# Spiking attention: score units of two full PSUM banks instead of two half-filled ones, clips and spikes dealt out anew over the engines

## The reference

```python
def spike(x):                      # THRE = 4
    return jnp.floor(jnp.clip(x, 0.0, THRE) + 0.5)
B, N, C = x.shape                  # 16, 548, 128
H = 8; hd = C // H; scale = hd ** (-0.5)
...                                # spike, Wqkv, batch norm over all tokens
q = spike(qkv[0]); k = spike(qkv[1]); v = spike(qkv[2])
attn = jnp.einsum('bhnd,bhmd->bhnm', q, k)
attn = spike(attn)
out = jnp.einsum('bhnm,bhmd->bhnd', attn, v) * scale
out = spike(out.transpose(0, 2, 1, 3).reshape(B, N, C))
return jnp.einsum('bnc,dc->bnd', out, Wproj) + bproj
```

## Time and profile before

| | before |
|---|---|
| median of three runs | 2126.67 us (2124.03 to 2128.3) |
| profiled execution, its own time | 2130.16 us |
| its span in the trace | 2128.3 us |
| PE, DVE, ACT, POOL busy over the span | 73%, 62%, 35%, 34% |
| `attend`: first instruction of the block to the last of the residual | 1246.6 to 1650.8 us |
| scores: first and last start | 1258.8 and 1646.7 us |

### The profile page before, as it was taken

The page is one execution under the profiler, slowest core; times in us unless marked ns, Lnnn a source line. Parts: engine busy times, 40 slices in busy tenths (PEclk is TensorE's granted clock), DMA queues, the critical chain, the costliest instruction groups (busy, mean ns, idle before and its releaser), DMA issues. The chain is left out here.

```text
span 2128.3 us, 31340 instructions
## 1 busy us (share of the span) xinstructions
PE 1544.4 (73%) x9132; PEld 1081.9 (51%) x9132; DVE 1318.0 (62%) x2105; ACT 744.3 (35%) x1369; POOL 719.1 (34%) x758
## 2 busy tenths in 40 slices
PE   5779999998701004776627558888888658999998
PEld 3457777775301003555514423333333457788787
DVE  3845555555577892111115777777777657989988
ACT  2235555555300001333203346677666321111111
POOL 1345555552000014788753012222231113323332
PEclk8679999999855556989858889999999859999999
DMA  4050000000210002444450000000000000000000
GB/s 137 0 232 1 0 0 0 0 0 0 74 32 0 1 1 52 85 78 81 64 150 28 4 2 2 0 0 0 0 0 0 1 32 8 11 11 15 11 15 14
DMA packets 69696, 60.85 MB, mean 29 GB/s; under 512 B 15789, under 2 KB 63675, under 8 KB 68363
## 3 DMA queue, kind: packets, MB, share of 16 engines
q1 hardware_dynamic: 52174, 47.52, 6.9%
q0 software_dynamic: 15744, 11.85, 4.1%
q10 hardware_dynamic: 1728, 0.85, 0.1%
HBM read 35.06 MB, written 25.18 MB: 28 GB/s over the span
## 5 line engine op out<-in xcount | busy, mean ns | idle before, releaser
L1610 DVE TENSOR_SCALAR at_clip<-at_slot 128x548 bf16<-128x548 f32 (+1 forms) x320 | 226.4, 722 | 79.7 <-PE at_slot L1453 72.8
L1541 ACT ACTIVATE at_clip<-at_slot,at_four 128x548 bf16<-128x548 f32 (+1 forms) x320 | 226.6, 713 | 126.9 <-PE at_slot L1453 125.0
L1453 PE MATMUL at_slot<-at_qm,at_ks 128*128 128x274 bf16 (+1 forms) x1280 | 216.9, 285 | 55.2 <-ACT at_clip L1541 45.7
L1591 POOL TENSOR_SCALAR at_qm<-at_qs,at_headmask 128x548 bf16<-128x548 bf16 x128 | 97.1, 777 | 360.6 <-DVE at_qs L1619 360.6
L1453 PEld LDWEIGHTS at_slot<-at_qm,at_ks 128*128 128x128 bf16 (+1 forms) x1280 | 90.7, 97 | 150.4 <-ACT at_clip L1541 90.7
L1188 DVE TENSOR_SCALAR ex_y<-ex_ps_y,ex_rows 128x128 f32<-128x128 f32 (+1 forms) x96 | 29.2, 346 | 216.2 <-PE ex_ps_y L1135 106.0
L467 PE MATMUL ga_kv<-ga_kern,ga_v 128*128 128x274 f32 x512 | 132.1, 400 | 14.3 <-ACT ga_kern L552 13.7
L2042 DVE TENSOR_REDUCE mx_routed<-mx_weighted 128x128 f32<-128x1024 f32 x69 | 137.6, 1995 | 2.4
L1092 POOL DMA_INDIRECT moe_sums<-ex_y,slot_sums x80 | 124.8, 1560 | 34.6 <-issue 21.3
L612 POOL TENSOR_TENSOR ga_rot<-ga_by_cos,ga_by_sin 128x274 f32<-128x274 f32 (+1 forms) x96 | 70.1, 730 | 168.0 <-DVE ga_by_sin L656 168.0
L1134 PE MATMUL ex_ps_y<-ex_down,ex_hid 128*128 128x128 f32 (+3 forms) x576 | 99.7, 325 | 34.3 <-ACT ex_hid L1175 22.2
(11 more groups left out here) (346 smaller groups left out, 3800.7 us busy)
## 6 DMA issues: line engine op xcount, KB each, us to landing
moe_sums<-ga_zeros SPq DMA_DIRECT2D x8, 1152.0 KB, 18.9
ar_rows<-moe_sums SPq DMA_DIRECT2D x32, 256.0 KB
ex_down<-in_down SPq DMA_DIRECT2D x32, 192.0 KB
out_h<-H SPq DMA_DIRECT2D x22, 192.0 KB, 1.9
H<-in_text SPq DMA_DIRECT2D x1, 4096.0 KB, 20.9
token_rows<-tr_rows SPq DMA_DIRECT2D x16, 256.0 KB
patches<-in_patches SPq DMA_DIRECT2D x1, 1728.0 KB, 7.8
ga_sin<-in_sin SPq DMA_DIRECT2D x1, 1644.0 KB, 10.2
```

The costliest lines, as they stand in the source:

```text
L1453: last = nc.tensor.matmul(slot[SLOT[T % 2][u]][0:rows_of(t), s, 0:HALF], ks[p][:, t * P:t * P + rows_of(t)], qm[p][:, h, j * HALF:(j + 1) ...
L1541: nc.scalar.activation(clip[T % 2][u][0:r], slot[SLOT[T % 2][u]][0:r, :, 0:HALF], ACT.Relu, bias=four[0:r], scale=-1.0).then_inc(by_act, 1)
L1591: last = nc.gpsimd.tensor_scalar(qm[p][:, h, :], qs[:], headmask[:, h:h + 1], 1.0, ALU.mult, ALU.mult)
L1610: nc.vector.tensor_scalar(clip[T % 2][u][0:r], slot[SLOT[T % 2][u]][0:r, :, 0:HALF], 4.0, None, ALU.min).then_inc(by_dve, 1)
```

## The change

All of it is in `attend`, except for a different release of semaphores after `load_inputs` and `gated_attention` (they are now cleared and freed on GpSimd after the block).

- A batch has eleven steps. Queries are cut at 256 and 512: steps 0 to 4 and 5 to 9 take 256 queries and one key tile each, step 10 takes the last 36 queries with all five key tiles. One score matmul now computes two heads, 2 x 256 = 512 columns, and fills a bank; a unit is two such matmuls, four heads, two full banks; a step has two units (half 0 and half 1) in the same three slots.
- DVE clips half 0 (heads 0 to 3), ACT half 1 (heads 4 to 7), one instruction of 1024 columns each per step (720 in step 10). There are three sets of `clip` buffers.
- The matmul with -4 is gone. Its sum is made by one DVE reduction of v per batch (`vsum`), which ACT adds as the bias of the output's relu, on channels 64 to 127.
- `weigh` is eight matmuls of 32 channels x 256 columns, forty of 36 columns in step 10.
- The spike: batch norm and relu (ACT, in place), then an add of 2^23 on GpSimd (`lift`), then min and subtract in one instruction (`settle`), on GpSimd for k and v, on DVE for q and the output. DVE loses five two-step spikes per batch and has three one-step ones.
- q, k, v, masks are made two batches ahead, in three sets. GpSimd's queue is written out for all 16 batches; the other engines' loop is over three batches, with seven batches written out in all (four before).
- Start: DVE sets the score and output banks and the value buffers to zero, and makes the eight masks of batch 0.

The diff, cut to its core:

```diff
         def _(pe):
-            def score(b, p, T, units, first=False):
...
-                    for s, h in enumerate(heads):
-                        last = nc.tensor.matmul(slot[SLOT[T % 2][u]][0:rows_of(t), s, 0:HALF], ks[p][:, t * P:t * P + rows_of(t)],
-                                                qm[p][:, h, j * HALF:(j + 1) * HALF], start=True, stop=True)
-                    last.then_inc(s_ps, 1)
+            def score(b, m, T, half, first=False):
+                n = STEPS * b + T
...
+                if not first:
+                    if half == 0:
+                        pe.wait_ge(by_act, n - 1)
+                    else:
+                        pe.wait_ge(by_dve, n)
+                to = slot[(m + 2 * T + half) % 3]
+                pe.sem_inc(met_pe, 1)
+                for g in (2 * half, 2 * half + 1):
+                    if T < 2 * KT:
+                        j, t = divmod(T, KT)
+                        last = nc.tensor.matmul(to[0:rows_of(t), g % 2, :].rearrange("p (s n) -> p s n", s=2), ks[m][:, t * P:t * P + rows_of(t)],
+                                                qm[m][:, 2 * g:2 * g + 2, j * QA:(j + 1) * QA], start=True, stop=True)
+                    else:
+                        for t in range(KT):
+                            last = nc.tensor.matmul(to[0:rows_of(t), g % 2, 2 * QR * t:2 * QR * (t + 1)].rearrange("p (s n) -> p s n", s=2),
+                                                    ks[m][:, t * P:t * P + rows_of(t)], qm[m][:, 2 * g:2 * g + 2, 2 * QA:S], start=True, stop=True)
+                last.then_inc(s_ps, 1)
...
-                nc.tensor.matmul(out_ps[j][:, 0:HALF], vo[p][0:r, t].rearrange("p h d -> p (h d)"), fours[0:r, :],
-                                 start=False, stop=False)
...
+            def steps_of(b, m, first, final):
+                for T in range(STEPS):
+                    if T + 1 < STEPS or not final:
+                        score(*ahead(b, m, T, 1), 1)
+                    if T + 2 < STEPS or not final:
+                        score(*ahead(b, m, T, 2), 0)
+                    weigh(b, m, T)
+                    if T == 3 and not first:
+                        project(b - 1, 1)
+                    if T == 7 and not final:
+                        turn_values(b + 1)
+                    if T == 9:
+                        project(b, 0, final)
...
         @block.scalar
+            def clip_high(b, m, T, first=False):
+                n = STEPS * b + T
+                act.wait_ge(s_ps, 2 * n + 2)
+                if not (first and T < 3):
+                    act.wait_ge(o_done, n - 2)
...
+            def steps_of(b, m, first, final):
+                for T in range(STEPS):
+                    clip_high(b, m, T, first)
+                    if T == 0 and not first:
+                        out_rectify(b - 1, (m + 2) % 3, 1)
+                    if T == 2 and not (isinstance(b, int) and b + 2 >= B):
+                        rectify(b + 2, Q, q_rect)
+                    if T == 3 and not (isinstance(b, int) and b + 2 >= B):
+                        rectify(b + 2, K, k_rect)
+                    if T == 5:
+                        out_rectify(b, m, 0)
+                    if T == 7 and not final:
+                        negative_values(b + 1, (m + 1) % 3)
+                    if T == 8 and not (isinstance(b, int) and b + 2 >= B):
+                        rectify(b + 2, V, v_rect)
...
         @block.gpsimd
+            for b in range(B):
+                if b + 1 < B:
+                    values(b + 1)
+                if b > 0:
+                    lift_out(b - 1, 1)
+                if b + 2 < B:
+                    lift_queries(b + 2)
+                    keys(b + 2)
+                    masks(b + 2, range(0, 4))
+                lift_out(b, 0)
+                if b + 2 < B:
+                    masks(b + 2, range(4, HEADS))
...
         @block.vector
+            def steps_of(b, m, first, final):
+                for T in range(STEPS):
+                    clip_low(b, m, T, first)
+                    if T == 2 and not first:
+                        settle_out(b - 1, 1)
+                    if T == 4 and not first:
+                        residual(b - 1, 1)
+                    if T == 5 and not (isinstance(b, int) and b + 2 >= B):
+                        settle_queries(b + 2)
+                    if T == 6 and not final:
+                        sum_values(b + 1, (m + 1) % 3)
+                    if T == 7 and not final:
+                        positive_values(b + 1, (m + 1) % 3)
+                    if T == 8:
+                        settle_out(b, 0)
+                    if T == 10:
+                        residual(b, 0)
...
+            nc.vector.memset(four[:], 4.0)
+            for m in range(3):
+                nc.vector.memset(vv[m][:], 0.0)
+                nc.vector.memset(vsum[m][:], 0.0)
+                nc.vector.memset(slot[m][:], 0.0)
+            for j in range(2):
+                nc.vector.memset(out_ps[j][:], 0.0)
+            nc.vector.tensor_scalar(up_scale[:], scale[:], UPWARD, None, ALU.mult)
+            nc.vector.tensor_scalar(up_shift[:], shift[:], UPWARD, None, ALU.mult).then_inc(ready, 1)
```

More of the change, by code:

```diff
@@ L1413, in attend @@
         four = sb("four", [P, 1])
+        up_scale = sb("up_scale", [P, 3])
+        up_shift = sb("up_shift", [P, 3])
         slot = [st.enter_context(nc.psum_tensor(f"at_slot{n}", [P, 2, 512], F32)) for n in range(3)]
         out_ps = [st.enter_context(nc.psum_tensor(f"at_out{j}", [P, 512], F32)) for j in range(2)]
[L1416 to L1419, removed]
@@ L1522, in _ @@
+            score(0, 0, 0, 1, True)
+            score(0, 0, 1, 0, True)
+            batches(pe, steps_of)
             project(B - 1, 1)
@@ L1525, in _ @@
         def _(act):
-            def rectify(b, n, first=False):
-                if not first:
-                    act.wait_ge(spiked, 3 * b + n - 2)
-                    act.sem_inc(met, 1)
-                c = WHERE[n]
-                nc.scalar.activation(relu[n][:], QKV[:, c, bass.ds(b * S, S)], ACT.Relu, bias=shift[:, c:c + 1],
-                                     scale=scale[:, c:c + 1]).then_inc(relu_done, 1)
-            def clip_odd(b, T, first=False):
-                TT = 10 * b + T
-                r = rows_of(T % 5)
-                for u in (1, 3):
-                    act.wait_ge(s_ps, 4 * TT + u + 1)
-                    if not first:
-                        act.wait_ge(o_done, TT - 1)
-                    nc.scalar.activation(clip[T % 2][u][0:r], slot[SLOT[T % 2][u]][0:r, :, 0:HALF], ACT.Relu,
-                                         bias=four[0:r], scale=-1.0).then_inc(by_act, 1)
@@ L1571, in _ @@
[L1571 to L1581 removed]
+            def clip_high(b, m, T, first=False):
+                n = STEPS * b + T
+                act.wait_ge(s_ps, 2 * n + 2)
+                if not (first and T < 3):
+                    act.wait_ge(o_done, n - 2)
+                of, to = slot[(m + 2 * T + 1) % 3], clip[(2 * m + T) % 3][1]
+                act.sem_inc(met_act, 1)
+                if T < 2 * KT:
+                    r = rows_of(T % KT)
+                    nc.scalar.activation(to[0:r], of[0:r], ACT.Relu, bias=four[0:r], scale=-1.0).then_inc(by_act, 1)
+                else:
+                    nc.scalar.activation(to[:, :, 0:2 * QR * KT], of[:, :, 0:2 * QR * KT], ACT.Relu, bias=four[:], scale=-1.0).then_inc(by_act, 1)
@@ new lines, in _, with lift, settle @@
+            act.wait_ge(ready, 1)
+            for b in range(2):
+                rectify(b, Q, q_rect)
+                rectify(b, K, k_rect)
+                rectify(b, V, v_rect)
+            negative_values(0, 0)
+            batches(act, steps_of)
+            out_rectify(B - 1, (B - 1) % 3, 1)
+        def lift(eng, dst, of, by):
+            return eng.tensor_scalar(dst, of, by, MAGIC, ALU.mult, ALU.add)
+        def settle(eng, dst, of):
+            return eng.tensor_scalar(dst, of, MAGIC + 4.0, MAGIC, ALU.min, ALU.subtract)
@@ L1583, in _, with mask @@
+        def mask(eng, m, h):
+            return eng.tensor_scalar(qm[m][:, h, :], qs[:], headmask[:, h:h + 1], 1.0, ALU.mult, ALU.mult)
         @block.gpsimd
         def _(pool):
[L1585 to L1592 removed]
@@ L1601, in _ @@
+            lift_out(B - 1, 1)
         @block.vector
         def _(dve):
[L1603 to L1611 removed]
```

361 lines of the change are left out of this document (170 added, 191 removed).

## The result

The changed kernel takes 2109.6 us (median of four runs, 2106.15 to 2114.23) against 2127.17 for the kernel before on the same chip: ratio 0.9923, 95% interval 0.9902 to 0.9943. So it is 17.5 us faster, inside the range of 2046 to 2112, but only a third of the 53 that were forecast. The profiled execution took 2110.86 us.

The account below looks back on a forecast made before the run. The prediction took a loop of waits between ACT's clip and PE's scores as the bound: 2130.16 minus 58 over 16 batches plus 5 gives 2077, or 2074 against the median 2126.67; range 2060 to 2090, wider 2046 to 2112.

Parts of the forecast that it names:

- The loop of waits: In attend, ACT's clip and PE's scores wait for each other, with weighing between: 2.47 us a step before the change.
- the old loop: The kernel before's cycle of scores, weighing and ACT clip in attend: 2.47 us a step, predicted to go.
- The pieces: Costs per step in attend: score unit 0.44 us, weighing 0.46, DVE clip 1.22, ACT clip 1.11.
- the first rival: Step 10's small matmuls don't overlap: its weighing 3.3 us instead of 1.1, +2.2 a batch, time 2110; chance 0.20.
- The three stalls: DVE waits for transposes behind clip 7, to 2.04, and for projections behind clips 10 and 4, 1.7 and 1.4 us.
- walk: One batch of attend followed operation by operation on PE, DVE and ACT: 20.7 us instead of 24.35, 58 us saved.
- the rival on the clock: PE idles 1.8 us behind step 7 and its clock falls; half clock gives 2300; slower by clock or GpSimd stalls 0.10.
- what would show it right: Signs in attend: GpSimd's masks 20.7 us apart, clips 1.22 and 1.11, PE idle until DVE's step 8 clips, clock 1.00.
- the table: Predicted end times of PE's steps and both clips through one batch, from DVE's clip 7 at 0 to 20.72 us.
- The start: Before attend's first score: longer memsets and the chain behind them make it about 4 us later than 12.2; together +5.
- a sign of being wrong: At attend's start, a first score more than 6 us later would show the prediction wrong.
- Costed at nothing: GpSimd's added work, 11.0 us of a 20.7 us batch, is free; the output's half 0 lift has 2.8 us cover.

Follow-up runs that it names:

- e7: The kernel before, without the matmul with -4 in each weighing: 2107.7 us, ratio 0.9902 to the kernel before.
- e3: The changed kernel with the value copies on DVE and ACT moved behind the next clip: 2066.1 us, ratio 0.9693 to the kernel before.
- e2: The changed kernel with PE's two projections one step earlier, behind steps 2 and 8: 2079.9 us, ratio 0.9763 to the kernel before.
- e1: The changed kernel with fourteen filling matmuls against zeros on PE behind the transposes of step 7: 2087.5 us, ratio 0.9798 to the kernel before.
- e5: e3 with the second half's projection after step 2 and DVE's first-half residual behind the next batch's first clip: 2036.0 us, ratio 0.9565 to before.
- e9: The changed kernel with GpSimd's settle of the keys multiplying by 1 instead of taking a minimum: 2116.6 us in one run.
- e8: e1 with GpSimd's lift of the output's first half after all eight masks instead of four: 2083.1 us, ratio 0.9797 to the kernel before.

## Why the prediction was right in direction and wrong in size

- **The loop of waits and its end: right.** e7 moves the old loop by 0.17 a step, and in the changed kernel ACT waits for scores 58.2 us of 315, not 101.6 of 335.
- **The pieces: right.** The clips take 1.22 and 1.11, the score matmuls 0.24 apart or less, eight weighing matmuls 0.33 from their start to the next scores. **Step 10's small matmuls overlap:** forty in 0.53 against 1.1 taken, so the first rival is wrong in its premise, and its time (2110) was hit by luck. The Trainium skill, "TensorE: Matmul & The Clock Gate", section "Wait — 56ns, not 53.3ns?", names about 62 ns per matmul where the hardware decoder is off, which by estimate would be 2.5 us for the forty. This trace, with 0.53, doesn't agree with that case; no run here shows which way the decoder stood.
- **The three stalls: right in place and size.** DVE waits 2.14 for the transposes (walk: 2.04), 1.45 and 1.26 for projections (1.7 and 1.4), PE idles 1.70 behind step 7 (1.8). e3 takes the first away and gains 1.6 us a batch, near the 1.8 of PE's idle time. e2 takes the other two away and gains 1.7 a batch, where DVE had waited 2.7 (walk: 3.1), so part of that wait cost nothing.
- **Where it failed: the clock.** The step is "Against it: 512-column matmuls stream at least as densely as now" in the rival on the clock, and "clock 1.00" in what would show it right. The walk itself had PE idle 1.8 us at a stretch, twice what the earlier trace rows shows for before, and no row of before showed the clock holding through such a gap. A mean of columns per microsecond says nothing on one gap. The rival's mechanism was true; its price was too high: it took the clock as half all the time (2300), where it falls for 3.4 or 6.8 us once a batch. By e1 this is 21.4 us of the shortfall, the largest part of it; without it (e1's 0.9798) some 43 us of the 53 are there. That 2109.6 still lies inside 2046 to 2112 is owed to the width of the range, not to the mechanism.
- **The walk was short by 0.8 us a batch.** An undisturbed batch is 21.43 to 21.56, not 20.7. From clip 7 (t = 0 at 1278.60) the trace stays within 0.25 us of the table until DVE's clip 1 (10.48, table 10.39), then falls behind in steps 2 to 6: clip 3 at 13.55 (13.12), 5 at 18.05 (17.46), 7 at 21.55 (20.72). The sum of v is 0.12 longer than taken (0.72); for the rest I only argue that two plain steps cost more than PE's 1.34, as e5's weighings 1.42 to 1.45 apart show where little else waits. Over the 14 full batches this is about 10 us.
- **The start: the sign right, 3 us too little.** The first score comes 7.1 us later, not 4, and past the 6 that the prediction had named as a sign of being wrong. The memsets cost 6.5, close to the 6 taken. The missing part is GpSimd's settle, 2.17 and 2.04 where 0.80 was taken from the earlier trace rows; these rows are float32 to float32, and by e9 it is not the minimum that makes the difference, which leaves the types. GpSimd does 8 x 0.73 + 3 x 0.65 + 2 x 2.04 + 0.85 = 12.7 us a batch instead of 11.0.

  ```profile
  1254.75 2.17 POOL L1606 TENSOR_SCALAR at_ks<-sa_qkv 128x548 bf16<-128x548 f32 x1
  ...
  1257.66 2.04 POOL L1606 TENSOR_SCALAR at_vs<-sa_qkv 128x548 bf16<-128x548 f32 x1
  1259.67 1.26 POOL L1602 TENSOR_SCALAR sa_qkv<-sa_qkv 128x548 f32<-128x548 f32 x2
  1260.50 0.73 DVE L1606 TENSOR_SCALAR at_qs<-sa_qkv 128x548 bf16<-128x548 f32 x1 [1.77 <-POOL sa_qkv L1602]
  ```

- **Costed at nothing: right for the lift.** e8 moves it by 2.8 us and changes nothing. At the start GpSimd's work did cost time, as the bullet above shows; what it costs in the middle of `attend` by slowing DVE's small operations no run separates.

The sum: 404.2 - 53 = 351.2 was forecast for `attend`, 384.7 came. The difference of 33.5 is 21.4 for the clock, 3.1 for the start and about 9 for the walk.

What stays open: which of PE's idle stretches decides over a fall. Batches with and without one show the same 1.70 us at the same place, e2 keeps that stretch and falls half as often, e7 falls with no stretch above 0.91, and e1 and e3 keep the clock with stretches up to 1.07. I have not varied the gap alone in steps.

## What to carry to other kernels

Walk the new order through, and then ask of each stall not only what waits for it but what it does to TensorE's clock: a saving that opens gaps on PE can be taken back by half, and it can be won again either by moving the waited-for work one step away (43 us from two moved operations) or, if nothing else helps, by filling the gap. A side task's result (transposes, a projection) should be taken up one clip later than it can be there. A short row of the same operation and size is no price if an operand's type differs.

## What was not expected of the hardware

- The clock of TensorE fell to half once a batch, for 3.4 or 6.8 us, with PE never idle longer than 1.7 us; with the gap filled (e1) or taken away (e3, e5), and PE's idle stretches at most 1.07 us, it stood at 1.00 through some 290 to 340 us. In e7 one matmul less per step was enough for ten falls, with PE never idle longer than 0.91 us.
- GpSimd: 548 columns float32 to bfloat16 take 2.04 us, float32 to float32 0.65, bfloat16 to bfloat16 0.72; the first is the same with a minimum and with a multiply (e9).
- Forty matmuls of 32 channels x 36 columns, with forty different weights, take 0.53 us together.
- While GpSimd runs masks, small DVE operations on SBUF can take more than twice as long: the same subtraction of 128 x 128 takes 0.29 at 1262.42, beside GpSimd's settle of the keys (1261.02 to 1263.13), and 0.73 at 1263.23, after the masks have started at 1263.11.

  ```profile
  1262.42 0.29 DVE L1759 TENSOR_TENSOR at_out_r<-at_out_r,at_w 128x128 f32<-128x128 f32 x1
  ...
  1263.11 3.54 POOL L1610 TENSOR_SCALAR at_qm<-at_qs,at_headmask 128x548 bf16<-128x548 bf16 x5
  1263.23 0.73 DVE L1759 TENSOR_TENSOR at_out_r<-at_out_r,at_w 128x128 f32<-128x128 f32 x1
  ```
